# Quantized attention products of an early-fusion block: the second chunk's Q/K products issued before the first V product, the image V groups placed between the text chunks

## The reference

```python
xq, _ = fq_act(x_s)
wq = fq_weight(w_s)
h = jnp.einsum('bnc,mc->bnm', xq, wq) + qkv_b
h, _ = fq_act(h)          # round(h / scale) + zero point, clipped to 0..255
qkv = h.reshape(B, N, 3, H, hd).transpose(2, 0, 3, 1, 4)
q, k, v = (qkv[0], qkv[1], qkv[2])
```

## Time and profile before

| what | us |
|---|---|
| runs, median of 3 (lowest to highest) | 1034.21 (1032.1 to 1034.34) |
| the profiled execution's own time | 1031.61 |
| its span, from the first to the last instruction | 1029.8 |
| stage `quant_qkv` in it, first matmul to end of the last DVE instruction | 165.10 to 225.34 |
| busy over the span: DVE / ACT / PE | 882.5 / 709.8 / 703.4 |

### The profile page before, as it was taken

The page is one execution under the profiler, slowest core; times in us unless marked ns, Lnnn a source line. Parts: engine busy times, 40 slices in busy tenths (PEclk is TensorE's granted clock), DMA queues, the critical chain, the costliest instruction groups (busy, mean ns, idle before and its releaser), DMA issues. The chain is left out here.

```text
span 1029.8 us, 22671 instructions
## 1 busy us (share of the span) xinstructions
PE 703.4 (68%) x5955; PEld 480.7 (47%) x5956; DVE 882.5 (86%) x2425; ACT 709.8 (69%) x1374; POOL 166.7 (16%) x274
## 2 busy tenths in 40 slices
PE   3873396747888366676667666666545286999997
PEld 3652244425555233343444433333233155889996
DVE  5898997888888799999999999999977874667766
ACT  0255475947888698898998998899955293545553
POOL 5851310017664000000000000000003530000000
PEclk9996598978999688787787888887856597999999
DMA  8000000001111111111111111111013004455452
GB/s 257 3 2 1 0 1 1 0 1 40 37 37 36 36 28 24 24 29 23 23 25 24 25 24 24 25 24 25 13 51 117 18 1 154 143 183 202 170 195 81
DMA packets 84271, 54.71 MB, mean 53 GB/s; under 512 B 53704, under 2 KB 83176, under 8 KB 83976
## 3 DMA queue, kind: packets, MB, share of 16 engines
q1 hardware_dynamic: 83208, 54.11, 17.3%
q0 software_dynamic: 1024, 0.13, 0.2%
HBM read 11.90 MB, written 3.76 MB: 15 GB/s over the span
## 5 line engine op out<-in xcount | busy, mean ns | idle before, releaser
L1357 DVE SCALAR_TENSOR_TENSOR expo<-expo,con,pow 128x153 f32<-128x153 f32 x480 | 146.2, 377 | 1.2 <-ACT expo L1266 1.2
L1140 PE MATMUL at_rem<-word,ident_half 128*128 128x459 f16 x160 | 65.8, 411 | 103.9 <-ACT expo L1266 102.1
L1266 ACT ACTIVATE expo<-at_rem,con 128x459 f32<-128x459 f32 x160 | 95.3, 639 | 14.1 <-PE at_rem L1141 13.2
L952 DVE TENSOR_REDUCE rs_ends<-rs_banks 128x770 f32 (+1 forms) x96 | 89.1, 958 | 12.5 <-PE rs_banks L924 10.0
L873 ACT ACTIVATE rs_banks<-rs_banks 128x770 f32<-128x770 f32 x96 | 74.3, 796 | 22.6 <-PE rs_banks L916 21.7
L1400 DVE CUSTOM_DVE_ANT_0 weight_top<-weight_top,line 128x2448 uint16<-128x2448 uint16 x64 | 86.2, 1346 | 2.1 <-ACT line L1258 2.1
L1222 ACT ACTIVATE word<-at_banks 128x459 uint8<-128x459 f32 x160 | 80.7, 560 | 10.1 <-PE at_banks L779 10.0
L1140 PEld LDWEIGHTS at_rem<-word,ident_half 128*128 128x128 f16 x160 | 15.7, 98 | 153.7 <-ACT expo L1266 148.1
L1258 ACT ACTIVATE line<-weight_top 128x1224 f32<-128x1224 f32 x64 | 74.0, 1158 | 15.1 <-DVE weight_top L1385 14.8
L774 PE MATMUL at_banks<-pick,row_top 128*128 128x459 bf16 x160 | 73.0, 456 | 11.5 <-ACT word L1222 4.7
L1930 ACT ACTIVATE qk<-e_p,b1s 128x153 f32<-128x153 f32 x192 | 58.7, 391 | 30.1 <-PE e_p L1891 28.9
(11 more groups left out here) (392 smaller groups left out, 2083.2 us busy)
## 6 DMA issues: line engine op xcount, KB each, us to landing
qk<-vt SPq DMA_DIRECT2D x64, 384.0 KB, 3.1
rs_kb<-qk SPq DMA_DIRECT2D x128, 28.7 KB, 1.9
kb<-qk SPq DMA_DIRECT2D x128, 28.7 KB, 1.9
patches<-in_patches SPq DMA_DIRECT2D x4, 768.0 KB
vi<-vt SPq DMA_DIRECT2D x32, 96.0 KB, 2.0
out<-vi SPq DMA_DIRECT2D x32, 96.0 KB, 1.7
pj_w<-in_w SPq DMA_DIRECT2D x1, 2304.0 KB, 8.2
qb<-qk SPq DMA_DIRECT2D x128, 6.0 KB, 1.8
```

What stands on the lines that cost most here:

```text
L952: v.tensor_reduce(ends[:, :, n, 5 * b:5 * b + 5], banks[:, slot(u, b), :, 0:5 * W].rearrange("p i (t n) -> p i t n", n=W), AX, ALU.max).th ...
L1140: pe.matmul(out, identh[:, :], bank(word, b).bitcast(F16), start=True, stop=False)
L1266: act.activation(bank(ex, b), rem[:, (u + b) % 2, 0:3 * N], ACT.Square, scale=2.0 ** 24, bias=c(5)).then_inc(sq_done, 1)
L1357: ins = v.scalar_tensor_tensor(ex[:, t, :], ex[:, t, :], c(7), pw[:, t, :].bitcast(BF16), ALU.add, ALU.mult, accum_out=tot[:, t:t + 1])
```

## The change

Three things are changed in `quant_qkv`; what is computed is the same, and the number of matmuls, activations and DVE operations too.

1. On PE the Q/K product of chunk 1 comes before the wait for `vrows` and the first V product. On DVE both `q_limit` of chunk 0 come before the wait for the diagonal products and the copies into `rows_v`.
2. The four image V groups move from behind the last chunk to behind chunks 2, 5, 8 and 11 (`AFTER`), on PE behind the Q/K product of the next chunk, on DVE behind `v_limit` of the chunk. The two slots of `pv` are taken in the order of turns (`turn_of`).
3. The loops over chunks on PE and DVE are written out, with fixed addresses. ACT keeps its loop.

```diff
-        def chunks(eng, body):
-            with eng.Fori(0, NCH // 2 - 1) as i:
...
+        AFTER = tuple(3 * g + 2 for g in range(G // 2))
+        image_of = lambda i: AFTER.index(i) if i in AFTER else None
+        turn_of = lambda i: i + sum(1 for x in AFTER if x < i)
...
-                def body(i, z):
-
-                    pe.wait_ge(vrows, 2)
-                    pe.wait_ge(v_scaled, i + 1)
-                    v_product(z, lambda w, kt: xqT[:, kt, ds(i * W + w * N, NT)])
-                    if not (isinstance(i, int) and i == NCH - 1):
+                def text_values(i):
+                    n = turn_of(i)
+                    pe.wait_ge(v_scaled, n + 1)
+                    v_product(n % 2, lambda w, kt: xqT[:, kt, i * W + w * N:i * W + w * N + NT])
+
+                def image_values(i, g):
+                    n = turn_of(i) + 1
+                    pe.wait_ge(v_scaled, n + 1)
+                    v_product(n % 2, lambda w, kt: xqI[:, kt, (2 * g + w) * P:(2 * g + w + 1) * P])
+
+                q_product(1)
+                pe.wait_ge(vrows, 2)
+                for i in range(NCH):
+                    text_values(i)
+                    if 0 < i < NCH - 1:
                         q_product(i + 1)
-                chunks(pe, body)
-                for g in range(G // 2):
-                    pe.wait_ge(v_scaled, NCH + g + 1)
-                    v_product(g % 2, lambda w, kt: xqI[:, kt, (2 * g + w) * P:(2 * g + w + 1) * P])
+                    if image_of(i) is not None:
+                        image_values(i, image_of(i))
...
+                for u in range(2):
+                    q_limit(0, u)
                 v.wait_ge(row_ps, 1)
...
-                chunks(v, body)
                 v.wait_ge(unit_set, 4)
-                for g in range(G // 2):
-                    v_scale(g % 2, NCH + g)
-                    v_shift(g % 2, NCH + g)
-                    v_limit(g % 2, NCH + g, ...)
+                for i in range(NCH):
+                    n = turn_of(i)
+                    if i > 0:
+                        q_limit(i, 0)
+                    v_scale(n % 2, n)
+                    if i > 0:
+                        q_limit(i, 1)
+                    v_shift(n % 2, n)
+                    v_limit(n % 2, n, ...)
+                    if image_of(i) is not None:
+                        g, n = image_of(i), n + 1
+                        v_scale(n % 2, n)
+                        v_shift(n % 2, n)
+                        v_limit(n % 2, n, ...)
```

More of the change, by code:

```diff
@@ L642, in q_product @@
                                 mm = pe.matmul(pq[:, u, t, 0:W], wqT[:, kt, (3 * u + t) * P:(3 * u + t + 1) * P],
-                                               xqT[:, kt, ds(i * W, W)], start=(kt == 0), stop=(kt == 1))
+                                               xqT[:, kt, i * W:(i + 1) * W], start=(kt == 0), stop=(kt == 1))
                         mm.then_inc(q_prod, 1)
@@ L702, in _, with q_limit @@
                     v.memset(unit[32 * j:32 * j + ID, :], 0.0).then_inc(unit_set, 1)
+                def q_limit(i, u):
+                    v.wait_ge(q_int, i * 2 + u + 3)
+                    v.tensor_scalar(qk[:, i * 2:i * 2 + 2, 3 * u:3 * u + 3, :].rearrange("p b t n -> p t b n"),
+                                    qi[:, u, :, :].rearrange("p t (b n) -> p t b n", n=N), cap, None, ALU.min).then_inc(q_done, 1)
+                for u in range(2):
+                    q_limit(0, u)
                 v.wait_ge(row_ps, 1)
@@ L708, in _ @@
                 both = lambda j: rows[:, j, :].unsqueeze(1).to_broadcast([P, 2, C])
[L710 to L713, removed]
                 def v_scale(z, n):
@@ L726, in v_limit @@
                     v.tensor_scalar(out, whole, cap, scale, ALU.min, ALU.mult).then_inc(v_done, 1)
[L728 to L733, removed]
-                chunks(v, body)
-                v.wait_ge(unit_set, 4)
-                for g in range(G // 2):
-                    v_scale(g % 2, NCH + g)
-                    v_shift(g % 2, NCH + g)
-                    v_limit(g % 2, NCH + g, vi[:, 2 * g:2 * g + 2, :].rearrange("p w (h f) -> p (w h) f", f=32)[:, :, 0:HD], unit[:, 0:1], False)
+                v.wait_ge(unit_set, 4)
+                for i in range(NCH):
[6 more added lines that the diff above has]
+                    v_shift(n % 2, n)
+                    v_limit(n % 2, n, vt[:, i * 2:i * 2 + 2, :].rearrange("p w (r x f) -> p (w r) x f", x=4, f=HD)[:, :, 0:4:3, :], V_UNIT, True)
+                    if image_of(i) is not None:
+                        g, n = image_of(i), n + 1
+                        v_scale(n % 2, n)
+                        v_shift(n % 2, n)
+                        v_limit(n % 2, n, vi[:, 2 * g:2 * g + 2, :].rearrange("p w (h f) -> p (w h) f", f=32)[:, :, 0:HD], unit[:, 0:1], False)
 class Stage:
```

## The result

The changed kernel takes **1029.91 us** (median of 5 runs, 1028.45 to 1030.89) against 1033.77 (median of 5, 1032.1 to 1034.34): the ratio is 0.9963, 95% interval 0.9949 to 0.9978, so 3.8 us faster, between 2.3 and 5.3. The forecast was 3.2 us faster, 1031.0. Measured once more, beside its parts, it came out at 0.9955 (0.9937 to 0.9973).

What follows compares the result with a forecast made beforehand. ACT was taken to set the pace of the chunks, standing idle at the stage's two ends. 5.90 + 1.59 - 0.49 - 3.80 = 3.2 us less, 1034.2 to 1031.0 us; likely 1029.7 to 1032.1, range 1028.2 to 1033.1.

Steps and rivals of the forecast that it cites:

- tail, behind ACT's completion: End of `quant_qkv`: the four image groups on DVE leave the stretch after ACT completes, 5.90 us gained.
- ACT starts chunk 1 earlier: Start of `quant_qkv`: ACT begins chunk 1 at 171.49 in place of 173.08, 1.59 us gained.
- first stall, ahead of chunk 2: ACT waits for `q_limit` of chunk 1, as the first V product comes later; 0.49 us lost.
- four groups: Each moved image group delays the next chunk's `q_limit` and stalls ACT 0.95 us; 3.80 us lost.
- The head: Start of `quant_qkv`, chunk 1's Q/K product and chunk 0's caps moved earlier: 1.59 us gained, 0.49 lost to a stall.
- Part 3: Writing out the PE and DVE chunk loops in `quant_qkv`: worth nothing by itself, since ACT set the pace.
- The fetch of new code: Rival: PE waits for written-out code in each of fifteen chunks, kernel 4.4 us slower, 1038.6; chance 0.05.
- DVE as the limit without stalls: Rival: in `quant_qkv` DVE runs without holding ACT up, gain 6.0 us, 1028.2; chance 0.12.
- Behind the stage: Rival: clock and phases of later stages fall differently, 1 to 3 us lost, 1033 to 1034; chance 0.12.
- a span of 1026.6: Whole kernel: an execution like the profiled one would take 1028.4 us, with this span.

Runs made afterwards that it cites:

- changed_again: The changed kernel, nothing altered, measured once more beside its parts; 0.9955 of the kernel before.
- experiment 9: Changed kernel with chunk 0's two `q_limit` put back behind the copies into `rows_v`, chunk 1's Q/K product staying ahead; 0.9968 of the kernel before.
- written_out: Kernel before with only the PE and DVE chunk loops written out, order of work kept; 0.9995 of the kernel before.
- images_only: Kernel before with loops written out and image groups moved behind chunks 2, 5, 8 and 11, start of stage unchanged; 0.9967 of the kernel before.
- four_qi: Changed kernel with four `qi` buffers in place of two; 0.9920 of the kernel before.
- busy_ahead: Changed kernel with 24 unread PE matmuls added at the end of the stage before (`range_h`); 0.9957 of the kernel before.
- spread: Changed kernel with each image group's three DVE steps spread between the next chunk's steps; 0.9931 of the kernel before.

## Why the prediction was right

The sum again, with `changed_again` against before, both with the diagonal products ended at 5.5:

| term | predicted | measured | from |
|---|---|---|---|
| tail, behind ACT's completion | 5.90 | 5.90 | 225.34 - 217.90 = 7.44; 221.24 - 219.70 = 1.54 |
| ACT starts chunk 1 earlier | 1.59 | 1.67 | 7.98 - 6.31 |
| first stall, ahead of chunk 2 | -0.49 | -0.44 | 9.72 - 6.31 - 2.97 |
| four groups | -3.80 | -3.39 | 84 activations in 45.22, unhindered 41.83 |
| sum | 3.20 | 3.74 | stage 60.24 - 56.48 = 3.76 |

- **The term that was mis-sized** is the four groups, 0.85 each in place of 0.95. The stalls themselves are as forecast: 0.91, and three times 0.94 to 0.95 (`changed_again`, from start to start), 3.75 together against 3.80. But ACT's completion is moved by less than its starts. Its last activation takes 0.70 behind the stalls and 0.94 at the end of 84 unhindered ones, which is 0.24, and the 0.12 left is spread over the run, whose steps are a little shorter. My sum had 0.73 for a last activation wherever it stood.
- **Some luck in one group.** From ACT's completion of a chunk to its release behind the group I had 3.69 and the trace has 184.00 - 180.29 = 3.71 (180.32 less the 0.03 of release). Two errors cancel in it: the cap starts at 2.93 and not at 2.97, and ACT starts 0.09 behind the cap's end (183.91), where I took 0.03.
- **The head** is right in what starts when. The copies started at 5.48 in the first profile, not at about 4.5, as the second cap stood ahead of them. That appears only where the clock rises early; experiment 9 shows it.
- **Part 3** was not quite nothing by itself: about 0.3 to 0.5 in the head, seen in the stage of `written_out` and not in the time. It lies between the copies and chunk 1's product, a path that part 1 takes out of ACT's way, so it doesn't come on top in the changed kernel: ACT starts chunk 1 2.50 behind the diagonal products before, 2.04 in `images_only` and 0.82 in `changed_again`. The fetch of new code, the rival that ended on the slower side, cost nothing that shows: `written_out` has no wait of PE or DVE without a recorded cause in the stage. The Trainium skill (Runtime: NRT & Kernel Launch, Instruction fetch mechanics) says that the next block of code is fetched while the current one runs. The waits of `written_out` agree.
- **DVE as the limit without stalls** (the first rival) did not come, and `four_qi` shows why: it needs the two further buffers. With them the stage is 7.4 us shorter and not 6.0, since DVE's text chunk takes 2.49 and not 2.61.
- **Behind the stage** nothing is given back that can be told apart: from the stage's end to the end of the span it is 803.6 to 806.1 us in all profiles, 804.5 before, 805.1 and 806.1 in the two of the changed kernel. The gain of the medians, 3.8, agrees with the stage's 3.76; single executions are too uneven to say more.
- My reading that an execution of the changed kernel like the profiled one would have a span of 1026.6 failed: it was 1029.1. The starts of the stage differ by 4.4 us between executions of kernels that are equal up to it, more than the whole gain. A forecast can be made for a stage in one execution, but must be tested in the median.

## What to carry to other kernels

Work moved from an idle tail into a busy stretch is not paid by its duration, but by how long it delays what the pacing engine waits for: here 0.85 of 1.48 a group. Take it apart so that each piece is shorter than the slack of the buffer ahead (0.1 a group), or give that buffer two more halves (nothing). And when several engines alternate over one buffer, follow one period from completion to release in the trace's own steps: that gave 0.95 a group, and the stalls measured 0.91 to 0.95.

## What was not expected of the hardware

- **PE's clock rises at different points of the same code.** At the stage's start it is at half, behind some 5 us in which PE did nothing; the diagonal products then end between 4.38 and 5.81 us into the stage in the profiles without `busy_ahead`'s matmuls, so their end moves by up to 1.4 us. With PE kept busy until 0.94 us ahead it is at full (3.40 and 3.39).
- **A DVE instruction starts 0.46 us behind a `v_scale` whose result it doesn't need, 0.58 behind one whose result it does** (180.06 to 180.64 in `four_qi`), though both find the same engine and a recorded duration of 0.55. That it is the result and not the kind of instruction shows in `spread`, where a `v_shift` of another slot follows a `v_scale`. Interleaving independent steps is itself worth 0.12 each.

```profile
182.50 0.55 DVE L724 TENSOR_TENSOR vf<-pv,rows_v 128x384 f32<-128x384 f32 x1
182.96 0.55 DVE L728 TENSOR_TENSOR v<-vf,rows_v 128x384 int16<-128x384 f32 x1
```

- **An activation takes longer the longer ACT has not been held up.** The first behind a wait takes 0.61, the twelfth 0.67, the eighteenth 0.70, and in `written_out` it grows to 0.94 and stays there, while the starts stay 0.49 to 0.51 apart. It is the same instruction in each (min/median/max in ns):

```profile
L688 ACT ACTIVATE qi<-pq,biasp,ap x96: 597/868/942, 165.7 to 214.2; 128x306 int16<-128x306 f32 x96
L688 ACT ACTIVATE qi<-pq,biasp,ap x96: 597/634/703, 166.5 to 219.0; 128x306 int16<-128x306 f32 x96
```

The first line is `written_out`, the second `changed_again`. The time counts for those who wait: a cap that finds DVE idle starts 0.03 behind the recorded end, whether the activation took 0.60 or 0.94. Why it grows is not shown by these runs.
- **So the idle that the profile shows for ACT understates a stall** by the overlap of two activations, which is not constant: 0.73 shown and 0.90 to 0.94 lost at the groups, nothing shown and 0.20 lost in `spread`. Count from start to start.
